# Attention to dense layer on one core: weight splits, the first gate and the last sums in another order

## The reference

```python
x = x + attention(layernorm(x))   # conv of width 3 to q, k, v of 256; 16 heads of 64, blocks of 128
                                  # tokens, causal; output 256 wide; @ proj_w (256x1024) + proj_b
x = x + dense(layernorm(x))

def dense(x):                                             # 4 active experts, rank 8
    y = x @ W_base.T + b_base                             # 1024 x 1024
    z = einsum('bth,erh->bter', x, lora_A[active])
    contribs = einsum('bter,eor->bteo', z, lora_B[active]) * 2.0
    logits = (x @ router_W.T + router_b)[..., active]
    alpha = softmax(log(domain_prior[active] + 1e-12) + logits)
    return y + einsum('bteo,bte->bto', contribs, alpha)
```

## Time and profile before

| | us |
|---|---|
| median of 3 runs | 824.88 |
| lowest, highest | 824.55, 827.91 |
| profiled execution: its own time | 826.53 |
| profiled execution: span, first to last instruction | 824.4 |
| TensorE busy in it | 790.7 (96%) |
| VectorE, ScalarE, GpSimd busy | 461.1, 408.1, 201.4 |

### The profile page before, as it was taken

The page is one execution under the profiler, slowest core; times in us unless marked ns, Lnnn a source line. Parts: engine busy times, 40 slices in busy tenths (PEclk is TensorE's granted clock), DMA queues, the critical chain, the costliest instruction groups (busy, mean ns, idle before and its releaser), DMA issues.

```text
span 824.4 us, 14321 instructions
## 1 busy us (share of the span) xinstructions
PE 790.7 (96%) x5248; PEld 703.9 (85%) x5248; DVE 461.1 (56%) x1357; ACT 408.1 (49%) x1085; POOL 201.4 (24%) x186
## 2 busy tenths in 40 slices
PE   3899999999999999999999999999979999999997
PEld 3798887777877888888888888888769999999996
DVE  6889966778877644333333335343664444544441
ACT  5953332344335997676768686867841111111110
POOL 2300103223330434252525252523220010101000
PEclk9999999999999999999999999999999999999999
DMA  8646833533446221212252321103132231313201
GB/s 332 239 125 176 262 121 116 207 120 112 147 140 242 98 90 39 104 39 99 95 220 104 83 86 54 54 27 128 59 92 91 93 97 58 103 52 103 69 35 52
DMA packets 41369, 94.03 MB, mean 114 GB/s; under 512 B 9299, under 2 KB 18387, under 8 KB 40020
## 3 DMA queue, kind: packets, MB, share of 16 engines
q1 hardware_dynamic: 38996, 84.73, 30.9%
q0 software_dynamic: 2304, 8.39, 2.5%
HBM read 66.63 MB, written 26.08 MB: 112 GB/s over the span
## 4 chain that ended last, share of the span: by engine, by line
PE 79%; DVE 11%; ACT 4%; issue 2%; POOL 2%; DMA 1%; SPq 0%; DVEq 0%; ACTq 0%
PE net_psum L63 15%; PE net_psum L65 15%; PE net_psum L64 15%; PE net_psum L1188 10%; PE net_psum L1255 5%; PE net_psum L1274 4%; PE net_psum L1266 4%; POOL raw L476 2%; PE net_psum L1172 2%; PE net_psum L1306 2%; PE net_psum L1307 2%; PE net_psum L1308 2%; PE net_psum L1320 2%; DVE raw L882 1%; DVE raw L883 1%
## 5 line engine op out<-in xcount | busy, mean ns | idle before, releaser
L63 PE MATMUL net_psum<-fw_hi,xT_hi 128*128 128x354 f32 (+1 forms) x384 | 125.6, 327 | 0.8 <-DVE xT_lo L1013 0.7
L64 PE MATMUL net_psum<-fw_lo,xT_hi 128*128 128x354 f32 (+1 forms) x384 | 124.5, 324 | 0.0
L65 PE MATMUL net_psum<-fw_hi,xT_lo 128*128 128x354 f32 (+1 forms) x384 | 124.5, 324 | 0.0
L493 POOL TENSOR_TENSOR pr<-pr,rrec 128x512 f32<-128x512 f32 x64 | 66.6, 1040 | 218.7 <-DVE rrec L949 218.7
L629 ACT ACTIVATE pr<-pr,negmax 128x128 f32<-128x128 f32 x256 | 99.2, 392 | 10.7 <-DVE negmax L956 10.7
L1188 PE MATMUL net_psum<-ua,wa 128*128 128x256 f32 x384 | 85.5, 385 | 2.4 <-DVE ua L840 2.4
L1188 PEld LDWEIGHTS net_psum<-ua,wa 128*128 128x128 f32 x384 | 73.7, 193 | 12.8 <-issue 2.6
L956 DVE CUSTOM_DVE_ANT_0 pr<-net_psum,mask 128x128 f32<-128x128 f32 x256 | 58.8, 286 | 45.2 <-PE net_psum L1255 45.2
L63 PE MATMUL net_psum<-x_hi,w_hi 128*128 128x512 f32 x192 | 77.0, 401 | 3.2 <-DVE w_lo L889 3.0
L476 POOL TENSOR_TENSOR raw<-raw 128x512 f32<-128x512 f32 x24 | 37.3, 1556 | 164.5 <-ACT raw L576 164.5
L63 PE MATMUL net_psum<-c_hi,wqk_hi 128*128 128x256 f32 x256 | 76.9, 300 | 0.0
(11 more groups left out here) (173 smaller groups left out, 1824.7 us busy)
## 6 DMA issues: line engine op xcount, KB each, us to landing
wa<-in_conv_w SPq DMA_DIRECT2D x24, 512.0 KB, 3.9
raw<-in_conv_w SPq DMA_DIRECT2D x24, 384.0 KB, 3.4
xn<-in_x SPq DMA_DIRECT2D x16, 512.0 KB, 10.6
xr<-in_x SPq DMA_DIRECT2D x8, 1024.0 KB, 5.0
x_scratch<-xr SPq DMA_DIRECT2D x8, 1024.0 KB, 4.0
x1t<-x_scratch SPq DMA_DIRECT2D x16, 512.0 KB, 4.1
out<-y POOLq DMA_DIRECT2D x16, 512.0 KB, 5.0
c_raw<-c_scratch SPq DMA_DIRECT2D x7, 768.0 KB, 4.8
```

Source lines behind the costliest of these rows:

```text
L63: pe.matmul(out, w_hi, x_hi, start=first, stop=False)
L64: pe.matmul(out, w_hi, x_lo, start=False, stop=False)
L65: return pe.matmul(out, w_lo, x_hi, start=False, stop=last)
L493: pool.tensor_tensor(pr[:, jj % 4], pr[:, jj % 4], rrec[:, jj % 4].unsqueeze(2).to_broadcast([P, UN, P]), ALU.mult).then_inc(s["p_ready"], 1)
```

## The change

- The splits of the W_base chunks that the dense layer takes first and second go from steps 64 and 65 to steps 60 and 61, and those behind them move up too; in step 67 the xT copies go ahead of a chunk, in step 68 three chunks become two. For this the memory rows of fw_hi, fw_lo and fw_raw are rotated by two (`row(c)`; the experts' and router's weights are rotated on the host), and fw_hi lies at the end of the arena, so that its last two rows fall on buffers that are free by then. x1t_2 and x1t_3 take its former place and are loaded in step 64 and not in step 60.
- Statistics and variance of tile 1 go to steps 52 and 53, its `tile_power` to step 54, its `tile_scale` to step 68.
- The first gate, with the logarithm and lsum, goes from behind step 70 to step 68, its exponential with it, ahead of a_hi and a_lo of the last group (step 69). The split of b goes to step 69.
- For the last group the sum of x and bias is done by VectorE (`last_bias`, in steps 69 and 71) and no longer by GpSimd.

```diff
@@ -155,7 +155,12 @@
...
     KB = 3 * ER + 2
+    SOON = 2
     XS = 4
+    def row(c):
+        return (c - SOON) % DC
@@ -224,7 +229,8 @@
...
         fw_raw, = place(nc, RAW, (("fw_raw", [P, DC, WZ], F32),))
-        fw_hi, x1t_2, x1t_3 = place(nc, SH, (("fw_hi", [P, DC, WZ], F32R), ("x1t_2", [P, DM], F32), ("x1t_3", [P, DM], F32)))
+        x1t_2, x1t_3 = place(nc, SH, (("x1t_2", [P, DM], F32), ("x1t_3", [P, DM], F32)))
+        fw_hi, = place(nc, CY + 2 * size_of([P, MC, GT]) - size_of([P, DC, WZ]), (("fw_hi", [P, DC, WZ], F32R),))
         x1t = (x1t_0, x1t_1, x1t_2, x1t_3)
@@ -399,7 +405,7 @@
...
                     for c in range(DC):
-                        sync.dma_start(fw_raw[:, c, Z:WZ], w_base[:, c]).then_inc(s["fw_loaded"], 16)
+                        sync.dma_start(fw_raw[:, row(c), Z:WZ], w_base[:, c]).then_inc(s["fw_loaded"], 16)
                 if (g, i) == (5, 0):
@@ -411,14 +417,10 @@
...
                         sync.dma_start(lbias[:, 1, e:e + 1], prior[bass.ds(expert, 1), :].to_broadcast([P, 1])).then_inc(s["lbias_loaded"], 16)
-                if (g, i) == (7, 4):
-                    sync.wait_ge(s["c_lo_ready"], 2 * (NG - 1))
-                    sync.wait_ge(s["v_done"], VT * (NG - 1))
-                    sync.wait_ge(s["qk_done"], NP * (NG - 1))
+                if (g, i) == (8, 0):
+                    sync.wait_ge(s["qk_done"], NJ)
                     load_tile(2)
                     load_tile(3)
-                if (g, i) == (8, 0):
-                    sync.wait_ge(s["qk_done"], NJ)
                     sync.wait_ge(s["v_done"], VT * NG)
@@ -495,15 +497,15 @@
...
                     c_low(g + 1, (i - 4) // 2)
-                if 0 <= g - 1 < NG and i in (5, 7):
+                if 0 <= g - 1 < NG - 1 and i in (5, 7):
                     k = (i - 5) // 2
...
                     pool.tensor_tensor(xr[:, k], xr[:, k], pb_r[:], ALU.add).then_inc(s["xb_ready"], 1)
-                if (g, i) == (6, 2):
-                    tile_power(0)
+                if (g, i) in ((6, 2), (6, 6)):
+                    tile_power((i - 2) // 4)
@@ -530,7 +532,7 @@
...
             for t in range(TT):
-                if t + 1 < TT:
+                if 0 < t and t + 1 < TT:
                     tile_power(t + 1)
@@ -691,9 +693,14 @@
...
             def high_dense(c):
-                act.wait_ge(s["qk_done"], NJ)
-                act.wait_ge(s["fw_loaded"], 16 * DC)
-                act.activation(fw_hi[:, c, Z:WZ], fw_raw[:, c, Z:WZ], ACT.Copy).then_inc(s["fw_hi_ready"], 1)
+                if c < SOON:
+                    act.wait_ge(s["qk_done"], NP * (NG - 1))
+                    act.wait_ge(s["v_done"], VT * (NG - 1))
+                    act.wait_ge(s["c_lo_ready"], 2 * (NG - 1))
+                    act.wait_ge(s["fw_loaded"], 16 * DC)
+                else:
+                    act.wait_ge(s["qk_done"], NJ)
+                act.activation(fw_hi[:, row(c), Z:WZ], fw_raw[:, row(c), Z:WZ], ACT.Copy).then_inc(s["fw_hi_ready"], 1)
@@ -702,29 +709,33 @@
...
+            def gate_exponential(t):
+                act.wait_ge(s["fmax_ready"], t + 1)
+                act.activation(expl[:], logit[:], ACT.Exp, bias=fnegmax[:], accum_out=esum[:]).then_inc(s["fexp_ready"], 1)
             def drain_step(J):
+                if J in (NJ - 4, NJ - 3):
+                    high_dense(J - (NJ - 4))
                 if J == NJ:
-                    high_dense(0)
+                    high_dense(2)
                 if J == NJ + 1:
-                    high_dense(1)
+                    high_dense(3)
                 if J == NJ + 2:
...
                     act.activation(fw_hi[:, :, ER:Z], r_raw[:].rearrange("p e c -> p c e"), ACT.Copy).then_inc(s["az_split_hi"], 1)
-                    high_dense(2)
-                    high_dense(3)
+                    high_dense(4)
                 if J == NJ + 3:
-                    high_dense(4)
                     tile_xT(0)
+                    high_dense(5)
                 if J == NJ + 4:
-                    high_dense(5)
                     high_dense(6)
                     high_dense(7)
-                if J == NJ + 5:
                     act.wait_ge(s["logp_in"], 1)
                     act.activation(logp[:], lbias[:, 1], ACT.Ln).then_inc(s["logp_ready"], 1)
-                if J == NJ + 6:
+                    gate_exponential(0)
+                if J == NJ + 5:
                     act.wait_ge(s["b_loaded"], 16 * (E_ACT + 1))
@@ -771,15 +782,13 @@
...
             attention_step(0, 2)
-            for J in range(HEAD, NJ):
-                attention_step(J // NP, J % NP)
-            for J in range(NJ, NJ + NP):
+            for J in range(HEAD, NJ + NP):
                 attention_step(J // NP, J % NP)
...
             for t in range(TT):
-                act.wait_ge(s["fmax_ready"], t + 1)
-                act.activation(expl[:], logit[:], ACT.Exp, bias=fnegmax[:], accum_out=esum[:]).then_inc(s["fexp_ready"], 1)
+                if t:
+                    gate_exponential(t)
                 act.wait_ge(s["azT_done"], t + 1)
@@ -1020,7 +1029,7 @@
...
                 dve.tensor_tensor(logit[:], zp[:, ER:Z], lsum[:], ALU.add).then_inc(s["logit_ready"], 1)
-                if t + 1 < TT:
+                if 0 < t < TT - 1:
                     variance(t + 1)
@@ -1047,7 +1056,7 @@
...
                 dve.wait_ge(s["fw_hi_ready"], c + 1)
-                dve.tensor_tensor(fw_lo[:, c, Z:WZ], fw_raw[:, c, Z:WZ], fw_hi[:, c, Z:WZ], ALU.subtract).then_inc(s["fw_lo_ready"], 1)
+                dve.tensor_tensor(fw_lo[:, row(c), Z:WZ], fw_raw[:, row(c), Z:WZ], fw_hi[:, row(c), Z:WZ], ALU.subtract).then_inc(s["fw_lo_ready"], 1)
@@ -1060,29 +1069,40 @@
...
                     dve.tensor_scalar(lbias[:, 1], lbias[:, 1], PRIOR_EPS, None, ALU.add).then_inc(s["logp_in"], 1)
+                if J == NJ - 12:
+                    tile_statistics(1)
+                if J == NJ - 11:
+                    variance(1)
+                if J in (NJ - 4, NJ - 3):
+                    low_dense(J - (NJ - 4))
                 if J == NJ:
-                    low_dense(0)
+                    low_dense(2)
                 if J == NJ + 1:
-                    low_dense(1)
+                    low_dense(3)
                 if J == NJ + 2:
...
                     dve.tensor_tensor(fw_lo[:, :, ER:Z], r_raw[:].rearrange("p e c -> p c e"), fw_hi[:, :, ER:Z], ALU.subtract).then_inc(s["az_split_lo"], 1)
-                    low_dense(2)
-                    low_dense(3)
+                    low_dense(4)
                 if J == NJ + 3:
-                    low_dense(4)
                     low_xT(0)
+                    low_dense(5)
                 if J == NJ + 4:
-                    low_dense(5)
                     low_dense(6)
                     low_dense(7)
-                if J == NJ + 5:
+                    tile_scale(1)
                     dve.wait_ge(s["logp_ready"], 1)
                     dve.tensor_tensor(lsum[:], logp[:], lbias[:, 0], ALU.add).then_inc(s["lsum_ready"], 1)
-                if J == NJ + 6:
+                    dve.wait_ge(s["lsum_ready"], 1)
+                    gate(0)
+                if J == NJ + 5:
                     dve.wait_ge(s["b_split_hi"], 1)
                     dve.tensor_tensor(b_lo[:], b_raw[:], b_hi[:], ALU.subtract).then_inc(s["b_split_lo"], 1)
+                    last_bias(0)
+            def last_bias(k):
+                dve.wait_ge(s["xr_loaded"], 16 * NG)
+                dve.tensor_tensor(xr[:, k], xr[:, k], pb_r[:], ALU.add).then_inc(s["xb_ready"], 1)
@@ -1142,18 +1162,18 @@
...
                 drain_step(J)
-            tile_statistics(1)
-            dve.wait_ge(s["lsum_ready"], 1)
-            gate(0)
             for J in range(NJ + NP - 1, NJ + NP + 3):
                 attention_step(J // NP, J % NP)
+                if J == NJ + NP - 1:
+                    last_bias(1)
             for t in range(TT):
...
                 if t + 1 < TT:
-                    tile_scale(t + 1)
+                    if t:
+                        tile_scale(t + 1)
                     low_xT(t + 1)
@@ -1337,7 +1357,7 @@
...
                     mm = three_pass(pe, yp[t % 2][b][:, 0:hi - lo], xT_hi[:, t % 2, c], xT_lo[:, t % 2, c],
-                                    fw_hi[:, c, lo:hi], fw_lo[:, c, lo:hi], c == 0, b == 0 and c == DC - 1)
+                                    fw_hi[:, row(c), lo:hi], fw_lo[:, row(c), lo:hi], c == 0, b == 0 and c == DC - 1)
                 if b == 0:
@@ -1415,9 +1435,9 @@
...
         "w_base": rows(ffn["W_base"].T), "b_base": ffn["b_base"].reshape(1, DM),
-        "lora_a": ffn["lora_A"].reshape(E_TOT, RANK, DC, P).transpose(0, 3, 2, 1),
+        "lora_a": np.roll(ffn["lora_A"].reshape(E_TOT, RANK, DC, P).transpose(0, 3, 2, 1), -2, 2),
         "lora_b": ffn["lora_B"].transpose(0, 2, 1),
-        "router_w": ffn["router_W"].reshape(E_TOT, DC, P).transpose(0, 2, 1),
```

(1 more changed line is left out.)

## The result

The changed kernel takes 821.47 us in the median of 8 runs (819.73 to 823.13); the kernel before, with the runs taken beside it, 825.30 (8 runs, 824.04 to 827.91). The ratio is 0.9946, with a 95% interval of 0.9929 to 0.9963. The forecast was 821.0. The profiled execution took 821.56 with a span of 819.7, against 826.53 and 824.4.

The account below looks back on a forecast made before the run. TensorE, busy 96% of the span, bounds the kernel; only its idle gaps can be won. 0.35 + 2.4 + 0.05 (restart behind the old gap) + 1.1 = 3.9 us earlier, from 824.88 to 821.0; range 819.5 to 823.8.

Parts of the forecast that it names:

- The loss in steps 61 to 64: Two weight splits moved to steps 60 and 61 delay VectorE's maximum, ScalarE's exponentials and TensorE: 1.1 us lost, bounds 0 and 4.4.
- The handover: Steps 66 to 68: earlier oT_lo and xT copies give 1.45 us back, so 0.35 won net of the 1.1 lost.
- The projections: Last group's projections: with gate and sums moved, the third starts right behind the second, without its gap; 2.4 us won.
- The x+bias term: Price of one x plus bias sum on VectorE before the third projection: taken as 1.17 us, bounds 1.17 and 2.39.
- The transposes: Tile 1's transposes before the dense tiles no longer wait for statistics, power and fxn, which lies ready early: 1.1 us won.
- The table loads: Two ScalarE loads ahead of the gate's exponential, 1.28 us each, ending in time; with the skill's drain, gain 1.4, not 3.9.
- The gaps: Four TensorE idle times between attention and dense tiles, 0.93, 0.69, 2.21 and 1.40 us: 5.2 us, the most to win.
- part 3: The gate and the sums of the last group: moving them removes the wait ahead of the third projection, 2.4 us won.
- rival E: Early splits, steps 60 to 63: subtractions stretched up to 1.93 us, 5.9 lost against 5.0 won, 825.8 us; chance 0.05.

Follow-up runs that it names:

- The gate late: Changed kernel with the first gate behind step 70 and its exponential behind the split of b, as before: 50.51 us from step 61's scores to the first 352-column block.
- the last kernel of the table: Changed kernel, early splits in steps 58 and 59, other six earlier, last group's sums on GpSimd behind the gate: 819.25 us, ratio 0.9909.

## Why the prediction was right

- **The loss in steps 61 to 64** was foretold as 1.1 (0.35 at the scores, 0.75 at Q and K) and was 0.9: the scores of step 63 came 0.17 late and Q and K 0.84, against step 61. Place and mechanism held; the term was 0.2 too large. ScalarE went through step 61 faster than my step-by-step copy of the row durations: a_hi started 5.9 behind the step's scores, where I had 6.2.
- **The handover** was foretold as 0.35 net; the first projection comes 0.40 earlier against step 61 (606.25 and 607.45 less 0.8). The 0.93 wait went, the dense layer started 0.7 earlier (foretold 0.6) and waited 0.36 for its last chunk. That this part fits so well is partly luck: the loss was 0.2 smaller than foretold, and what came back behind it was smaller too (1.3 for 1.45).
- **The projections**: 2.4 foretold, 2.4 measured (the third comes 2.73 behind the first, no longer 5.10). The x+bias term was 1.17 and is 1.21. The gate late gives 1.4 of it back; the other 1.0 was not taken apart (tile 1's statistics, which VectorE did ahead of the gate, stayed early in that kernel).
- **The transposes**: 1.1 foretold, 1.2 measured (1.35 from the azs transpose to the mark, was 2.52).
- **The table loads** took 1.28 each, the second from 600.86 and the exponential at 602.29; no drain was seen, so the estimate of 1.4 by the Trainium skill's figure (ScalarE: Activation LUTs, "What ACT_TABLE_LOAD costs") did not come.
- **Sum**: 3.9 foretold, 4.0 from step 61 to the mark, 3.8 between the medians.

One reading of the prediction was wrong beside this. The gaps were put at 5.2, "the most there is to win"; the 0.53 of step 67 was left out, and the last kernel of the table wins 6.0.

One step of the prediction failed without costing it: part 3 said of the sums, "Taken away from GpSimd it frees nothing that anyone waits for." With the gate moved to 601.9, GpSimd's sums would run beside it, and its scaling and its cast would stand until they end (1.47 and 2.10 us). I had looked at when the sums are needed, and not at what runs beside them. Before the change they ended at 606.8 and the gate began at 609.8, so none of the rows showed the harm. The trace had a small sign of it, a sum of 4 columns out of SBUF that ends with GpSimd's work at 606.8 and takes 0.35, where the changed kernel has 0.16:

```profile
606.49 0.35 DVE L1082 TENSOR_TENSOR lsum<-logp,lbias 128x4 f32<-128x4 f32 x1
```

The same holds for rival E: GpSimd's contention was weighed for the early splits, where it does not arise, and not for the gate. The Trainium skill (GPSIMD Engine Reference, "Specifications") lists contention with two SBUF inputs or a mode of two ports. The two-input rows agree; the cast, copy and scaling are held as well, and the trace does not tell in which mode they run.

## What to carry to other kernels

Take the queue of each engine as a timetable, with every wait as an arrow: here seven of ten edits came out within the range it gave, two with splits in steps 58 and 59 were 0.2 and 0.3 us slower than it, and it missed by 3.9 us (2.4 when repeated) the one in which GpSimd ran beside the VectorE instructions of the gate. Move work out of the step in which a queue has its extra work (here a_hi and a_lo in step 61); two steps earlier the two splits cost 0.3 and no longer 0.9; idle time that looks alike in every row is not alike in the next step. And before an instruction is moved in time, list what GpSimd does in its new place: a short VectorE instruction can be held there for nearly the whole length of a GpSimd one.

## What the runs showed of the hardware

- Beside a GpSimd tensor_tensor with two SBUF inputs, a VectorE cast, copy, tensor_scalar or tensor_tensor whose inputs are all in SBUF was held until GpSimd's ended: 0.18 us of work took up to 2.32, and 0.22 took 2.41. One input in PSUM: 0.68 to 0.69, with or without. Not every kind is held: a reciprocal took its 0.17 beside GpSimd in both executions with the sums at their old time, and a reduction its 0.16 in the one where it fell beside them. Where VectorE was at work when GpSimd's instruction was issued (L69, L74), GpSimd's own took 3.38 and 2.84 for 2.35.
- TensorE's clock behind a wait of about 2 us: 0.51 for 3.4 us once, 1.00 once, and 1.00 behind the 2.21 us before the change. What decides is open.
- The granted clock between 10 and 30 us was 0.85 to 1.00 in single executions; counted from TensorE's first instruction, the highest (the kernel with splits in 62 and 63, 1.00) reached step 61 at 1.7 us ahead of the kernel before (0.94), the lowest (0.85 and 0.86) 1.4 to 1.5 behind. These two rows are of the kernels with splits in 62 and 63 and with the splits as before (columns as above):

```profile
10.00:30.00 20.00, 13.99 (x83) 12.69 (x84) 16.20 (x40) 18.17 (x23) 6.27 (x12) 1.00 1.01 395
```

```profile
10.00:30.00 20.00, 13.65 (x71) 12.35 (x72) 14.57 (x38) 16.90 (x20) 5.39 (x10) 0.86 1.01 394
```

TensorE gets through 83 matmuls in the first and 71 in the second. The clock is not all of it: at 0.91 step 61 came 553.4 behind the first instruction in the changed kernel (76 matmuls in these 20 us) and 552.4 in the one with the sums on GpSimd behind the gate (81). What sets it is open. From 30 to 560 us the clock was 1.00 in both and in the kernel before. So a change of 4 us is better read between two marks behind this stretch than from single times.
